# VectorE's side work moved behind the key features and the low part of the transposed output

## The reference, cut to what matters

```python
x = x + 0.5 * _L0_ffn_ref(_layernorm(x), ...)       # mixture of 8 experts, top 2, layer norm of its output
x = x + _L0_attn_ref(_layernorm(x), ...)            # linear attention, 16 heads of 64
x = x + 0.5 * _L0_ffn_ref(_layernorm(x), ...)       # the same mixture again
# attention, for token t and head h, with relu and cos/sin weights of the position:
#   S += k v^T (cos and sin part), z += k
#   out = (q S) / max(q z, 1e-6);  then out @ Wo + bo
# feed-forward: softmax over 8 logits, top 2, renormed; gelu(x Wup^T) Wdown^T; layer norm; + x
```

## Time and profile before

| what | value |
|---|---|
| median of 3 runs | 1253.76 us (1251.31 to 1256.22) |
| profiled execution, own time | 1257.42 us |
| its span | 1255.5 us |
| attention, DVE's first to last L1258 | 289.5 to 992.8 us of the span |
| DVE busy over the span | 1009.6 us (80%) |
| L1238 in the attention, 63 of them | 1250 ns on the mean |
| a step without a piece in block 0 | 9.2 us |
| busy in 363 to 735 us: DVE, PE, ACT, POOL | 334.03, 311.29, 236.42, 240.27 us of 372 |
| busy in 735 to 822 us: DVE, PE, ACT, POOL | 78.94, 76.26, 60.09, 51.48 us of 87 |

### The profile page before, as it was taken

The page is one execution under the profiler, slowest core; times in us unless marked ns, Lnnn a source line. Parts: engine busy times, 40 slices in busy tenths (PEclk is TensorE's granted clock), DMA queues, the critical chain, the costliest instruction groups (busy, mean ns, idle before and its releaser), DMA issues.

```text
span 1255.5 us, 32918 instructions
## 1 busy us (share of the span) xinstructions
PE 928.8 (74%) x12872; PEld 752.7 (60%) x12872; DVE 1009.6 (80%) x2109; ACT 707.3 (56%) x1014; POOL 765.9 (61%) x635
## 2 busy tenths in 40 slices
PE   3303988878988878878878988978979778859800
PEld 3302977766766656656656766756766667748700
DVE  7887786987889899899899898898888768538923
ACT  2112766657765755666765776746757646636600
POOL 2178736706867656757656565557987721767264
PEclk9999999989999998999999999988989989969955
DMA  9322424310000000000000000000000012234231
GB/s 336 128 109 73 141 79 111 103 47 6 8 9 8 8 6 8 8 7 8 8 6 2 2 2 2 2 2 19 14 14 13 21 53 72 95 97 122 77 93 50
DMA packets 69508, 61.77 MB, mean 49 GB/s; under 512 B 8304, under 2 KB 60016, under 8 KB 69104
## 3 DMA queue, kind: packets, MB, share of 16 engines
q1 hardware_dynamic: 60448, 42.64, 11.1%
q0 software_dynamic: 8192, 16.79, 4.3%
q10 hardware_dynamic: 720, 0.23, 0.1%
HBM read 30.80 MB, written 28.84 MB: 48 GB/s over the span
## 4 chain that ended last, share of the span: by engine, by line
DVE 30%; POOL 25%; PE 20%; issue 16%; ACT 6%; DMA 2%; DVEq 0%; POOLq 0%; SPq 0%
POOL xs L636 8%; POOL arena_a L1377 5%; DVE arena_b L1275 4%; POOL arena_a L1359 4%; DVE arena_a L1233 3%; PE bank L1043 3%; DVE arena_c L828 3%; ACT arena_c L1153 3%; POOL arena_b L665 2%; DVE arena_c L1271 2%; POOL arena_c L1381 2%; DVE xn_new L426 2%; DVE arena_b L1258 2%; PE bank L742 2%; DVE zt L705 2%
## 5 line engine op out<-in xcount | busy, mean ns | idle before, releaser
L636 POOL DMA_INDIRECT xs<-xhl,slot_idx x128 | 154.1, 1204 | 98.3 <-issue 57.2
L803 ACT ACTIVATE arena_c<-bank,s_pre 128x1024 f32<-128x1024 f32 x92 | 102.3, 1112 | 164.4 <-PE bank L744 158.9
L1377 POOL TENSOR_TENSOR arena_a<-arena_a 128x1024 f16<-128x1024 f32 x64 | 139.4, 2178 | 53.5 <-ACT arena_a L1153 52.9
L1359 POOL TENSOR_TENSOR arena_a<-arena_b,trig_rows 128x512 f32<-128x512 f32 x128 | 160.3, 1272 | 8.6 <-issue 8.6
L1153 ACT ACTIVATE arena_c<-arena_a 128x1024 f16<-128x1024 f32 x64 | 67.6, 1057 | 161.5 <-DVE arena_a L1233 161.5
L757 PE MATMUL bank<-wdn_hi,arena_c 128*128 x736 | 131.2, 222 | 31.8 <-DVE arena_c L828 31.8
L665 POOL DMA_INDIRECT arena_b<-ys,slot_idx x96 | 108.5, 1130 | 66.5 <-DMA ys<-arena_b 38.8
L828 DVE SCALAR_TENSOR_TENSOR arena_c<-arena_c,s_h 128x1024 f16<-128x1024 f32 x92 | 125.2, 1361 | 22.1 <-ACT arena_c L808 22.1
L758 PE MATMUL bank<-wdn_hi,arena_c 128*128 x736 | 131.2, 222 | 0.0
L759 PE MATMUL bank<-wdn_lo,arena_c 128*128 x736 | 131.0, 222 | 0.0
L1258 DVE TENSOR_TENSOR arena_b<-bank,decay 128x512 f32<-128x512 f32 x128 | 82.4, 686 | 41.0 <-PE bank L1043 40.4
(11 more groups left out here) (227 smaller groups left out, 3762.8 us busy)
## 6 DMA issues: line engine op xcount, KB each, us to landing
arena_b<-xs SPq DMA_DIRECT2D x92, 128.0 KB
ys<-arena_b SPq DMA_DIRECT2D x92, 128.0 KB
xs<-arena_c SPq DMA_DIRECT2D x2, 3072.0 KB, 18.2
arena_a<-in_w_up SPq DMA_DIRECT2D x1, 2048.0 KB, 13.0
arena_b<-in_w_down SPq DMA_DIRECT2D x1, 2048.0 KB, 13.6
xs<-xhl,slot_idx POOLq DMA_INDIRECT x128, 2.3
out_x<-x_tok SPq DMA_DIRECT2D x8, 256.0 KB, 2.7
arena_b<-ys,slot_idx POOLq DMA_INDIRECT x96
```

The source lines that it names most:

```text
L636: nc.gpsimd.indirect_dma_start(d["xs"][half], bass.IndirectOffsetOnAxis(slot_idx[:, half, choice, t:t + 1], axis=0), xhl[:, half, t, :], N ...
L1359: i = nc.gpsimd.tensor_tensor(q_trig[h], q_relu[h], trig_rows[:, bass.ds(u * BLK, BLK)], ALU.mult)
L1377: nc.gpsimd.tensor_tensor(q_lo, arena_a[:, 0:2 * BLK], q_hi, ALU.subtract).then_inc(a["q_lo_done"], 1)
```

## The change

`beside(n, hp)` is called later in DVE's step: not between L1275 and L1233 but behind L1242, ahead of the denominators. The routing of block 6 is taken out of it and keeps its old place. No instruction is added or removed; PE's, ACT's, POOL's and SP's programs stay as they are. Two lines more in the file make L1286, L1289 and L1291 of before L1288, L1291 and L1293 of the changed kernel.

```diff
                 v.wait_ge(a["probs_hi_done"], 2 * s + 2)
                 nc.vector.tensor_tensor(probs_lo, probs, probs_hi, ALU.subtract).then_inc(a["probs_lo_done"], 1)
-                beside(n, hp)
+                if n == 6 and hp == 0:
+                    route(v, 2)
                 ahead(n, u, hp, lambda u_, to: k_features(u_, to, s + 1))
                 if hp:
                     out_low(s - 1)
@@
                     if n > 0:
                         out_low(last_step(n - 1))
 
+                beside(n, hp)
                 out = ps_so[:, :, 0:TPB * VZ].rearrange("p h (c z) -> p h c z", c=TPB)
                 v.wait_ge(a["o_done"], s + 1)
@@
                 if n == 5:
                     for j in ((0,), (), (1, 2), (3, 4), (5, 6), (7,), (8,), (9,))[hp]:
                         gating(v, 2, j)
-                if n == 6 and hp == 0:
-                    route(v, 2)
```

## The result

The changed kernel takes 1288.89 us (median of 6 runs, 1284.3 to 1292.16), the kernel before 1254.87 us beside it (6 runs, 1251.31 to 1258.95): a ratio of 1.0257, 95% interval 1.0231 to 1.0284. That is 34 us slower, where 18 were forecast and the range ended at 1288. Where some executions of a kernel lay over 1.5% above its fastest, ratios leave them out and medians do not. The profiled execution took 1289.64 us, with a span of 1287.8 us.

What follows compares the result with a forecast made beforehand. It took each attention step to be bound by a ring over four engines, DVE the busiest. Step terms +19.7, clock +3, long waits -5 gave +17.7, say +18: median 1272 us, own range 1260 to 1284, full range 1256 to 1288.

Steps and rivals of the forecast that it cites:

- the decisive term: In steps with a piece, DVE reaches L1238 only inside POOL's L1377 and is held; head pair 6 ends at +11.9.
- hp 2, blocks 1 to 5 and 7: Head pair 2: L1377 comes late, so L1275 is held too, some 0.7 us; +9.0 us in all.
- hp 3, blocks 1 to 4: Head pair 3: L705 and L710 need 2.75 us behind L1359 instead of 4.4; -3.6 us in all.
- block 5, hp 3 to 7: Five steps with short gating pieces all reach L1238 after +8.70: 61.9 us instead of 51.71, +10.2.
- L1238 is held by L1377: DVE reaches L1238 at +9.5, inside POOL's L1377, and is held until +10.83, ending 1.09 us later.
- L1238 is not held: Rival, chance 0.10: L1377 starts later or lets L1238 pass, steps cost 11.07 instead of 11.9; 1253 us, no change.
- The 0.77 us at L1233 come back: DVE's wait for PE's key projection, formerly covered by the piece, shows again at L1233: 0.77 us per step with four L426.
- the pieces get shorter: At +6.25 only POOL's second L1359 is left, so four L426 cost 2.15 us instead of 2.7.
- hp 4, +4.0: Head pair 4, blocks 1 to 4: short piece, L1238 meets L419 or L1377; step 9.91 to 11.0 us, +4.0 in all.
- TensorE's clock: PE idles ahead of scores and state products; three more steps lose about 1 us each: +3, bounds 0 and 8.
- The long waits, -5: The L414 of 5.44 us moves past the POOL run it lost to: -5; the two long L1275 stay.
- more runs lost: Rival, chance 0.22: L1275 in head pairs 1 and 2 loses to whole POOL runs, 5 us each; three more make 1287.
- Steps without a piece keep 9.2 to 9.7 us: Sign to check in the changed kernel: attention steps with no piece of side work should stay at 9.2 to 9.7 us.

Runs made afterwards that it cites:

- e12: Changed kernel in which POOL's L1377 also waits until L1238 is done: 1335.31 us, ratio 1.0012, stretch 692.4 us.
- e1: Kernel before with POOL's L1377 cut from 1024 to 128 columns, most of the queries' low part left out: 1329.57 us, ratio 0.9892, stretch 683.8 us.
- e2: Changed kernel with POOL's L1377 cut from 1024 to 128 columns: 1328.2 us, ratio 0.9888, stretch 679.6 us.
- e8: Changed kernel with idle products that nothing reads added to PE's queue where it waits: 1342.41 us, ratio 1.0051, stretch 712.6 us.
- e5: The changed kernel itself run again, on another chip: 1382.01 us, ratio 1.0378 to the kernel before, stretch 736.9 us.
- e6: Changed kernel with L1238 issued ahead of the piece and the denominators: 1511.49 us, ratio 1.1318, stretch 874.7 us.
- e10: Each piece at its cheapest place: most ahead of L1275, some as in the changed kernel or the kernel before: 1315.31 us, stretch 675.4 us.
- e7: Kernel before with the piece moved earlier, ahead of L1275 and behind the low sums: 1331.27 us, ratio 0.9966, stretch 691.6 us.

## Why the prediction was right in direction and too small by nearly half

The direction and the decisive term were right; the size was off by 16 us in the median and 14 in the stretch. The steps' own lengths give the account, forecast and then measured, in us:

| term | forecast | measured |
|---|---|---|
| hp 6, blocks 1 to 4 | +5.2 | +4.6 |
| hp 2, blocks 1 to 5 and 7 | +9.0 | +11.4, of which block 7 +3.8 |
| hp 4, blocks 1 to 4 | +4.0 | +3.8 |
| hp 3, blocks 1 to 4 | -3.6 | -0.8 |
| hp 0, blocks 1 to 4 | -3.6 | -5.8 |
| hp 1, blocks 1 to 6 | -1.5 | +0.1 |
| block 5, hp 3 to 7 | +10.2 | +15.8 |
| clock, in steps not listed above (hp 7 of blocks 1 to 4, hp 3 of block 7) | +3 | +6.4 |
| the long L414 of block 7 | -5 | -3.4 |
| hp 0 of blocks 5 and 6, hp 2 of block 6 | 0 | -0.1 |
| sum | +17.7 | +32.0 |

- *L1238 is held by L1377*: right, in mechanism and price. L1238's mean rose to 1.64 us, hp 6 took 11.89 us, and e12, e1 and e2 show that the whole loss hangs on it. It was held in 18 steps. The rival "L1238 is not held" is what e12 made true, and it gave more than its 1253, which is no change: the stretch is 10 us shorter, 9 of them at the long waits, of which the rival had counted one.
- *The 0.77 us at L1233 come back, the pieces get shorter*: right (0.77 and 2.12 us in the rows above).
- *hp 4, +4.0*: met by luck. The reason given was that L1238 meets the power L419 or L1377, and it meets neither: it takes 1.22 to 1.24 us in all four. What costs there is the clock, 2.6 to 3.4 us at the lower level in three of the four steps, so that DVE waits for PE at L1233; in e8 all four take 10.20 us, together what they took before. Block 3, hp 4 of the changed kernel:

```profile
616.94 1.29 DVE L1233 SCALAR_TENSOR_TENSOR arena_a<-bank,trig_cols 128x512 f32<-128x512 f32 x2 [1.56 <-PE bank L969]
...
621.23 1.23 DVE L1238 TENSOR_TENSOR arena_c<-arena_a,arena_c 128x1024 f16<-128x1024 f32 x1
```

- *TensorE's clock, "three more steps with about 1 us lost", bounds 0 and 8*: this is the step that failed. I had seen the halved clock in one step of before and priced it for steps that wait as long as that one. But PE waits in the held steps, for the output and then for L1238; the clock was lower for a time in the step behind 16 of the 18, and in block 5 five such steps stand in a row. e8 measures it as some 20 us, and there the reckoning without it is met: block 5's five steps take 61.7 us for 61.9. Of these 20 the kernel before had up to 5, its longer waits at L1258, so that some 15 or more stand where +3 stood. The rows of the table in which it shows are hp 3, hp 4, block 5 and hp 7.
- *The long waits, -5*: wrong in the sum. Of the three, the L414 of 5.44 us fell to 2.82, the L1275 of 7.43 us in block 6 went away too but its piece was held for 4.97 us in its place, the one in block 2 stayed, and in block 7, hp 2, L1238 took 3.88 us. By the lengths of these four steps it comes to -1.4 us. The rival "more runs lost" had the time, 1287, for another reason than the one measured: there were not three more.
- *Steps without a piece keep 9.2 to 9.7 us*: some were longer in the kernel before already, up to 10.5 us. They kept their length in block 0, in hp 5 of blocks 1 to 4 and from hp 3 on in block 6, and not in hp 7 of blocks 1 to 3 (11.2 to 11.5) and hp 3 of block 7 (10.71 for 9.21), behind a held step.

What stays open: how the 44 us between e5 and e12 divide into the hold itself, the clock behind it and the long waits, of which block 2's alone is 4.4. e8 gives some 20 for the clock; what the idle products cost in e8 is not known.

## What to carry to other kernels

Before side work of VectorE is moved, look at which instruction with two inputs in SBUF gets behind it and what GpSimd will be running by then: of two queues that hold each other up, the one with time to spare should be made to wait, which was worth 42 to 44 us of the stretch here. Price a delay that TensorE waits out twice, once for itself and once for the slow stretch behind it, which shows as idle time of another engine in the next step: here L1238 grew by 24.7 us and the lower clock cost some 20. Side work is cheapest where GpSimd is idle: the same four instructions took 2.77, 2.12 and 1.11 us in three places.

## What the runs showed of the hardware

- A granted clock that halves behind a wait can cost as much as the wait or more. The hold of 1.3 us in block 3, hp 6 made its step 1.2 us longer than before and the next one 1.7; it left PE busy 1.85 of 4 us, and the next 4 us ran at 0.70 and 0.50; in e12 PE was busy 2.42 of the 4 us that answer to it, and the clock stayed at 1.00. The stretch's mean clock was 0.93 in the changed kernel, 0.97 in e12 and 0.88 in e6.
- The hold goes both ways. In e10 POOL's L1385, a low part of 130 columns, started at 651.41 inside DVE's L1277, and took 1.17 us; the same instruction takes 0.42 in the changed kernel's block 3, hp 6:

```profile
651.41 1.17 POOL L1385 TENSOR_TENSOR arena_c<-arena_c 128x130 f16<-128x130 f32 x1 [2.09 <-ACT arena_c L1203]
```

- A held L1238 ended 1.08 to 1.09 us behind the POOL instruction's end in all 18 held steps of the changed kernel and in block 0 of e6, with L1377 and with L1359 alike, though it takes 1.22 to 1.27 us alone. The Trainium skill (SBUF — State Buffer, "Who interferes with whom") says that the other engine is fully blocked until the first one's instruction is done; the trace agrees on who waits and until about when, but what is left of L1238 behind it is 0.14 to 0.19 us less than a full one.
- A waiting engine can lose to a whole run of instructions and not to one: 4.04 us in e7 for an L414 that takes 0.17 alone. Why one instruction loses to the whole run and another gets through after the first, no run here shows.
